# A quantised FFN pipeline on one core: the FFN2 product scaled by VectorE alone, the low parts of x formed on GpSimd

## The reference

```python
def fake_quant_lastdim(x):
    s = jnp.maximum(jnp.max(jnp.abs(x), axis=-1, keepdims=True) / 127.0, 1e-08)
    return jnp.clip(jnp.round(x / s), -127.0, 127.0) * s

def dyn_quant_linear(x, w, b):
    return jnp.einsum('bti,oi->bto', fake_quant_lastdim(x), fake_quant_lastdim(w)) + b

y = jnp.einsum('bij,bkj->bik', x, weight[adapter_ids])      # adapter, in fp32 accuracy
h = layernorm(y, gamma, beta)
h = dyn_quant_linear(h, w1, b1)                             # FFN1
h = jax.nn.gelu(h, approximate=False)
h = dyn_quant_linear(h, w3, b3)                             # FFN2
out = x + h
```

## Time and profile before

| | us |
|---|---|
| median of 3 runs | 415.48 |
| lowest, highest | 414.76, 419.6 |
| span of the profiled execution, first to last instruction | 413.9 |
| busy in it: TensorE | 349.4 |
| VectorE | 355.9 |
| GpSimd | 291.2 |
| ScalarE | 228.8 |
| mean granted clock of TensorE, as a share of full speed | 0.937 |

### The profile page before, as it was taken

How to read it: one execution, slowest core, us unless ns; L and a number is a source line. 1 busy time by engine, 2 the same in 40 slices (tenths; PEclk the granted TensorE clock), 3 DMA queues, 4 the chain that set the end, 5 groups by cost and what they waited for, 6 DMA issues and landing times.

```text
span 413.9 us, 5331 instructions
## 1 busy us (share of the span) xinstructions
PE 349.4 (84%) x1735; PEld 236.8 (57%) x1752; DVE 355.9 (86%) x320; ACT 228.8 (55%) x220; POOL 291.2 (70%) x143
## 2 busy tenths in 40 slices
PE   4999486889969898898799987999699969999755
PEld 4788364557545655666375745666475737575322
DVE  1987699889859998999899989999899979966796
ACT  3399463647547285546817474549635782735331
POOL 1414038244599859976599689996899689995970
PEclk9999868989998989899999996999899998999969
DMA  7999981459556984388906994589617991170112
GB/s 251 383 392 238 217 248 29 109 118 247 110 101 136 300 175 101 77 187 265 175 5 140 302 172 95 101 213 265 130 35 153 313 185 26 51 254 1 51 52 101
DMA packets 78616, 67.32 MB, mean 163 GB/s; under 512 B 3078, under 2 KB 71686, under 8 KB 78602
## 3 DMA queue, kind: packets, MB, share of 16 engines
q1 hardware_dynamic: 78602, 67.14, 64.7%
HBM read 58.74 MB, written 8.39 MB: 162 GB/s over the span
## 4 chain that ended last, share of the span: by engine, by line
POOL 34%; issue 9%; DVE 5%; ACT 2%; PE 1%; POOLq 0%
POOL o L427 7%; POOL y L418 7%; POOL x_res L437 6%; POOL a L443 6%; POOL y L420 4%; POOL o L431 2%; DVE a L902 2%; ACT y L545 2%; PE y_ps L1012 1%; POOL rstd L408 1%; POOL y L499 1%; DVE a L898 1%; POOL y L497 1%; POOL var_eps L404 0%; DVE g_half_max L907 0%
## 5 line engine op out<-in xcount | busy, mean ns | idle before, releaser
L994 PE MATMUL y_ps<-w_hi,x_hi 128*128 128x512 f32 x256 | 111.3, 435 | 29.9 <-DVE x_lo L753 18.1
L996 PE MATMUL y_ps<-w_hi,x_lo 128*128 128x512 f32 x256 | 105.9, 414 | 0.0
L995 PE MATMUL y_ps<-w_lo,x_hi 128*128 128x512 f32 x256 | 105.9, 414 | 0.0
L731 DVE TENSOR_TENSOR w_lo<-w_t,w_hi 128x2048 fp32r<-128x2048 f32 x28 | 93.0, 3322 | 6.5 <-ACT w_hi L512 6.3
L1012 PE MATMUL y_ps<-w_q,q_t 128*128 128x512 bf16 x369 | 85.3, 384 | 6.7 <-ACT q_t L562 4.6
L994 PEld LDWEIGHTS y_ps<-w_hi,x_hi 128*128 128x128 f32 x256 | 52.1, 204 | 47.2 <-issue 28.3
L725 DVE STREAM_TRANSPOSE w_t<-w_nat 128x2048 f32<-128x2048 f32 x28 | 64.5, 2305 | 5.1 <-DMA w_nat<-in_L_cond_weight 4.4
L1012 PEld LDWEIGHTS y_ps<-w_q,q_t 128*128 128x128 bf16 x384 | 36.5, 99 | 49.1 <-issue 9.1
L512 ACT ACTIVATE w_hi<-w_t 128x2048 fp32r<-128x2048 f32 x28 | 53.6, 1913 | 16.0 <-DVE w_t L725 16.0
L996 PEld LDWEIGHTS y_ps<-w_hi,x_lo 128*128 128x128 f32 x256 | 51.5, 201 | 11.9
L995 PEld LDWEIGHTS y_ps<-w_lo,x_hi 128*128 128x128 f32 x256 | 52.0, 203 | 10.7 <-issue 0.5
(11 more groups left out here) (107 smaller groups left out, 460.7 us busy)
## 6 DMA issues: line engine op xcount, KB each, us to landing
w_nat<-in_L_cond_weight SPq DMA_DIRECT2D x112, 256.0 KB, 4.7
x_res<-in_x SPq DMA_DIRECT2D x7, 1024.0 KB, 8.5
out<-o SPq DMA_DIRECT2D x14, 512.0 KB, 6.2
w_nat<-in_x SPq DMA_DIRECT2D x24, 256.0 KB, 5.8
w_nat<-in_L_cond_weight SPq DMA_DIRECT2D x8, 512.0 KB, 8.2
w_q<-in_L_ffn_w SPq DMA_DIRECT2D x4, 512.0 KB, 9.9
o<-in_L_ffn_w SPq DMA_DIRECT2D x4, 512.0 KB, 9.9
o<-in_x SPq DMA_DIRECT2D x2, 512.0 KB, 4.5
```

Of the source, the lines that this page charges most:

```text
L731: dve.tensor_tensor(w_lo[:, u], w_t[:, u % 2], w_hi[:, u].bitcast(F32), ALU.subtract).then_inc(w_lo_ready, 1)
L994: pe.matmul(ps, hi, w_hi[:, u, c], start=begin, stop=False)
L995: pe.matmul(ps, hi, w_lo[:, u, c], start=False, stop=False)
L996: last = pe.matmul(ps, lo, w_hi[:, u, c], start=False, stop=end)
```

## The change

FFN2's product leaves PSUM by one VectorE operation that multiplies by the token's scale and by the row of w3's scales. ScalarE's step and GpSimd's multiplication are gone, and with them one semaphore. The low parts of x go from VectorE to GpSimd, both halves of the item's input behind the `normalisers`.

```diff
 # GpSimd
             def finish(f):
                 for t in range(TT):
                     n = TT * f + t + 1
                     pool.wait_ge(ffn2_scaled, n)
-                    pool.tensor_tensor(o[:, t, :], o[:, t, :], w_scale_row[:, 1, :], ALU.mult
-                                       ).then_inc(out_scaled, 1)
-                    pool.wait_ge(out_scaled, n)
                     pool.wait_ge(x_b3_ready, n)
                     pool.tensor_tensor(o[:, t, :], o[:, t, :], x_res[:, t, :], ALU.add).then_inc(out_ready, 1)
+            def low_x(b):
+                for ch in range(CH):
+                    half = slice(CU * ch, CU * (ch + 1))
+                    pool.wait_ge(x_hi_ready, HALVES * (b - 1) + ch + 1)
+                    pool.tensor_tensor(x_lo[:, half], (x_t_1 if is_second(b) else x_t)[:, half],
+                                       x_hi[:, half].bitcast(F32), ALU.subtract).then_inc(x_lo_ready, 1)
...
                 normalisers(b)
+                if not (isinstance(b, int) and b == B - 1):
+                    low_x(b + 1)
...
             round_prep(3)
+            low_x(1)
             normalisers(0)
 # VectorE
+            def scale_ffn2(f, t):
+                if is_first(f):
+                    dve.wait_ge(scale_row_ready, 2)
+                dve.wait_ge(ffn2_done, KH * (TT * f + t + 1))
+                wait_past(dve, stored[t], 16 * f)
+                dve.scalar_tensor_tensor(o[:, t, :].rearrange("p (h k) -> p h k", k=BANK), y_ps[:, t],
+                                         g_scale[:, t:t + 1],
+                                         w_scale_row[:, 1, :].rearrange("p (h k) -> p h k", k=BANK),
+                                         ALU.mult, ALU.mult).then_inc(ffn2_scaled, 1)
...
                 mean_and_variance(1)
-                low_x(2, 0)
+                scale_ffn2(0, 0)
                 transpose_w(2, 1)
-                low_x(2, 1)
                 low_w(2, 1)
+                scale_ffn2(0, 1)
...
                     transpose_x(b + 1)
-                    low_x(b + 1, 0)
+                scale_ffn2(f, 0)
+                if not last:
                     low_w(b + 1, 1)
-                    low_x(b + 1, 1)
+                    scale_ffn2(f, 1)
```

More of the change, by code:

```diff
@@ L190, in adaln_ffn_kernel @@
         ffn2_scaled = sem("ffn2_scaled")
-        out_scaled = sem("out_scaled")
         out_ready = sem("out_ready")
@@ L572, in gelu @@
                 act.activation(a[:, t, :], a[:, t, :], ACT.Gelu).then_inc(g_ready, 1)
[L574 to L579, removed]
             def round_prep(part):
@@ L618, in second_iteration @@
                 split_x(2, 1)
-                scale_ffn2(0, 0)
                 normalise(1)
                 split_w(2, 1)
-                scale_ffn2(0, 1)
             def iteration(b):
@@ L649, in iteration @@
                     split_x(b + 1, 0)
-                scale_ffn2(f, 0)
                 if not last:
@@ L653, in iteration @@
                     split_x(b + 1, 1)
-                    scale_ffn2(f, 1)
             def last_ffn():
@@ L673, in last_ffn @@
                 take_halves(0, h_transposed, TT * f + 1)
-                scale_ffn2(f - 1, 1)
                 take_halves(1, h_transposed, TT * f + 2)
@@ L748, in transpose_x @@
                               src.rearrange("p sb (c r) -> p sb c r", r=BLK)).then_inc(x_transposed, 1)
[L750 to L754, removed]
             def statistics(b, kh):
@@ L928, in last_ffn @@
                                       ).then_inc(h_rounded, 1)
+                    if t == 0:
+                        scale_ffn2(f - 1, 1)
                 rescale_and_bias(0)
@@ L962, in _ @@
             low_w(1, 0)
-            low_x(1, 0)
             transpose_w(1, 1)
-            low_x(1, 1)
             statistics(0, 1)
```

## The result

| | before | changed |
|---|---|---|
| median, us (4 runs each) | 415.98 | 423.5 |
| lowest, highest | 414.76, 419.6 | 421.62, 424.47 |
| profiled execution: time; span | 414.76; 413.9 | 421.62; 419.8 |

The changed kernel takes 1.0201 of the time before, 95% interval 1.0159 to 1.0243: slower by 2.0%, clear of no change, while the interval leaves open whether it is more or less than 2%. The spans of the changed kernel's other three runs are 422.1, 422.6 and 421.2, so the profiled one is its fastest.

The account below looks back on a forecast made before the run. No engine is full; a loop of waits through all engines bounds the kernel. Terms -0.6 + 1.3 + 2.0 + 1.9 + 1.2 + 3.7 = +9.5 give span 423.4, time 425.0 us, range 417.4 to 432.0.

Parts of the forecast that it names:

- iteration 7, to the last statistics: Last loop iteration: no low part of its own, but h comes as late; +1.2 us.
- rival (b): Milder: b3 adds all fall well, the end costs half or nothing; +3.9 to +5.7, 419.4 to 421.2 us; chance 0.33.
- The walk through one iteration: Loop iteration, timed from its x transpose (T): late h makes VectorE wait, next transpose at 45.8 instead of 45.3 us.
- Rival (a): VectorE's saved 3.3 us per iteration are gained, if h is in time: 16.5 us less, 399; chance 0.08.
- The edge, +1.9: Iteration's end: w_lo may lose the port to the second b3 add; +1.9 us, counted in one of four iterations.
- The four iterations, +0.5 each: Four loop iterations: 45.8 us each against 45.3, +2.0 us in all.
- The first, +1.3: First loop iteration: low parts first come between shift and gamma; +1.3 us, between 0 and 4.7.
- The prologue, -0.6: Ahead of the loop: item 1's low parts go to an idle GpSimd; -0.6 us, between -2.4 and +1.2.
- The end, +3.7: After the last statistics (U 0): VectorE waits for TensorE's FFN2 ahead of the last gamma step; +3.7 us, between 2.2 and 4.0.

Follow-up runs that it names:

- e2: Changed kernel with the product back on ScalarE and GpSimd, low parts of x staying on GpSimd: 429.03 us, ratio 1.0351 to the kernel before.
- e7: Changed kernel without the addition of beta for items 0 to 6, so part of the computation is missing: 407.66 us, ratio 0.9851 to the kernel before.
- e8: Changed kernel with the second low part of x formed twice on GpSimd: 436.3 us, ratio 1.054 to the kernel before.
- e6: Changed kernel with x transpose ahead of the last statistics, x_hi ahead of w_hi(1), first low part ahead of the normalisers: 420.66 us, ratio 1.0152.
- e11: e10 with e6's order, the x transpose ahead of the last statistics: 417.09 us, ratio 1.0056 to the kernel before.
- e3: Changed kernel with item 6's first product moved behind the rounding of the last item's tile 0: 419.29 us, ratio 1.012 to the kernel before.
- e1: Changed kernel with the low parts of x back on VectorE, the product staying there: 421.03 us, ratio 1.0155 to the kernel before.
- e12: e1 with item 6's first product moved behind the rounding of the last item's tile 0: 417.38 us, ratio 1.0069 to the kernel before.
- e9: e6 with e3's end, item 6's first product behind the rounding of the last tile 0: 416.86 us, ratio 1.0062 to the kernel before.
- e5: Changed kernel with w's transpose and w_lo moved into VectorE's wait for h, ScalarE's split of that w ahead of rounding h: 424.88 us, ratio 1.0218.
- e10: e3 with gamma and beta of tile 0 of items 1 to 6 as two VectorE operations behind the x transpose: median 410.8 us, six runs.
- e13: e10 with the first product ahead of the two new VectorE operations: 415.05 us, ratio 1.0006 to the kernel before.

## Why the prediction was right

The direction and the mechanism held: VectorE's saved time turned into its wait for h, and the end cost about 3 us. The size (2.0% for 2.3%) held in the sum only, and partly by luck. The pieces, changed against before, in the two profiled executions:

| piece | predicted | measured |
|---|---|---|
| to the x transpose of item 2 | -0.6 | +1.7 (107.12 - 105.41) |
| first loop iteration | +1.3 | -0.3 |
| the four iterations | +2.0 and +1.9 | +0.8 |
| iteration 7, to the last statistics | +1.2 | +1.0 |
| the end | +3.7 | +2.7 |
| sum | +9.5 | +5.9 |

The medians are 7.5 apart, the profiled execution of the changed kernel being its fastest; the traces' 5.9 is nearer to rival (b)'s upper figure, +5.7, than to the forecast's 9.5. Of these 5.9, 1.7 lie in the prologue, where the forecast had -0.6. The pieces from the x transpose of item 2 to the last statistics were to cost 6.4 and cost 1.5.

The working began with GpSimd's 34% of the chain. That chain covers 51% of the span only, so the figure can't bear much; no term of the sum rests on it.

**The walk through one iteration was right nearly step by step.** TensorE's start at T 8.2: measured 8.0. h of tile 0 at 15.2 and of tile 1 at 20.0: 15.0 and 19.9. w_lo until 24.6, then the transpose: 24.3. w_lo asked for at 41.6: 41.2. Next transpose 45.8: 45.0 here, 45.5 in the mean. It could be right because what it rests on held in these rows to about 0.1 us: an operation with two SBUF inputs and one of GpSimd's alternate, each at full speed. The subtraction, which no row showed, costs what its lower bound said: of the 5.85 us for two, 1.3 pass before w_lo ends at about 251.66, which leaves 2.3 each. The product took no part in the alternation: the second one, from 251.57 to 252.85, lies beside GpSimd's low part and takes 1.28, the first, with GpSimd idle, 1.24. The rule of the Trainium skill that the prediction weighed (SBUF — State Buffer, "Who interferes with whom") says the same, and the trace agrees.

**Rival (a)** wanted h by T 14.5 and 18.5. It came 0.5 and 1.4 us late, and the 3.3 us saved went into the 8.17 us wait. e2, e7 and e8 showed that this wait follows GpSimd's list; e6 and e11 that TensorE's start isn't the limit.

**The edge, +1.9, didn't fall**: mis-sized, it measured 0. In the iteration shown w_lo came 0.15 us ahead of the end of the first b3 add, in the other three 1.5, 0.5 and 0.6 us, and it got the port next each time. I had the add start 9.05 us after x_res is issued; it was 9.99, 8.66, 8.67 and 9.05. A term that hangs on such a time is a chance, not a sum. Rival (b) was right in this one point.

**The four iterations, +0.5 each**, measured +0.2. **The first, +1.3**, didn't come; I had cut down an upper bound of 4.7 without a row for what covers it. This iteration spreads from 45.0 to 49.5 us among these kernels.

**The prologue, -0.6**: the sign isn't confirmed. The x transpose of item 2 stands at 107.12, but at 103.95 in e3's trace, whose program is the same up to there; a difference of 0.6 can't be seen against that. The prologue alone wasn't run.

**The end, +3.7** between 2.2 and 4.0, measured +2.7. The wait of 2.4 was 2.23, and the inversion that was to end at U 24.6 ended at 24.3. But the way there was another, and that the figure fits is luck. I had `L902` of tile 0 alternate with GpSimd as before (2.07 each); they took 0.69, and in their place stood the 1.31 and 1.68 us for TensorE at the lower clock, which I had not thought of. Behind the inversion I had TensorE's part unable to shrink from 7.4. It took 5.6 (404.44 to 410.07): the granted clock was 1.00 there, 0.63 before (398 to 405, behind an idle time of 4.39 us). With the 0.77 us that TensorE then waits for VectorE, its last transposes stand at U 30.7 instead of the forecast's 32.0 (28.0 before). `L902` of tile 1 took 0.69, as forecast, though the 2.07 it was set against is a row of tile 0.

What this place in the list costs is shown three times by moving one line, by the time from the last statistics to the end of the span: 3.0 us (39.7 - 36.7), 3.3 (e1 to e12) and 3.1 (e6 to e9); the medians of the last two pairs are 3.6 and 3.8 apart. It is about half of the change's cost, and it is no property of the product, only of its place ahead of the last gamma step.

## What to carry to other kernels

Before moving an operation to a less busy engine, write down that engine's list and ask what stands behind the new place and when it is wanted: about 5 us of work ahead of h took back all that VectorE saved, although both engines' busy times fell. Where engines exclude each other on a port, count the port users up to the result that is waited for, whichever engine they run on. Filling the wait with one of them didn't pay (e5); taking two off GpSimd paid in e10 and, less, in e13, but not in e11, where VectorE's own list had become the longer one. And look at the last item apart from the loop: a step that is hidden in the loop may stand in the open there.

## What was unexpected of the hardware

Which of two operations issued within 0.05 us of each other goes first can change from one iteration to the next: in e10 VectorE's beta operation took 1.28 us in three iterations of the loop and 3.48 in one, and GpSimd's two low parts 7.9 or 5.6. Even GpSimd's 128x2 operations take part in the alternation: behind a VectorE operation with two inputs, one that takes 0.19 us was recorded at 1.22 in e3. And programs that are the same up to the x transpose of item 2 reached it 3.2 us apart (103.95 in e3, 107.12 in the changed kernel), more than most of the terms that were to be measured.
